# Two decoder layers on one core: products of zeros in TensorE's waits at the seams, a new order for the first stage, and gathers moved ahead at the third stage's start

## What is computed

```
x = x + gated(layernorm(x))                    # layer 0: 1x1 convolutions, 4-tap convolution, silu, softplus
x = x + cross(q=layernorm(x), k=v=ctx)         # 16 heads of 16
x = x + moe32(layernorm(x))                    # 32 experts, top 2, at most 154 rows each, gelu, 256 -> 1024 -> 256
x = x + causal(layernorm(x))                   # layer 1: 16 heads, softmax twice with an entropy-dependent temperature
x = x + mixed(layernorm(x), ctx, phi)          # one head of 256 with a bias from phi
x = x + block(layernorm(x))                    # rms norm, rotary attention, then 8 experts, top 2
```

```python
pos_all = jnp.cumsum(oh, axis=0) - 1
pos = jnp.take_along_axis(pos_all, flat_e[:, None], axis=1)[:, 0]
valid = pos < C
he = jax.nn.gelu(jnp.einsum('ecd,edf->ecf', xe, w1) + b1[:, None, :], approximate=False)
ye = jnp.einsum('ecf,efd->ecd', he, w2) + b2[:, None, :]
y = (y_flat.reshape(T, K, D) * w[..., None]).sum(axis=1)
```

## Time and profile before

| | us |
|---|---|
| median of three runs | 1469.34 (1469.23 to 1470.68) |
| the profiled execution, its own time | 1475.01 |
| its span | 1473.2 |
| TensorE products busy in the span | 1298.6 (88%) |
| TensorE weight loads | 981.8 (67%) |
| VectorE | 781.4 (53%) |
| ScalarE | 687.2 (47%) |
| GpSimd | 534.0 (36%) |
| stage A / barrier into B / barrier into C | 0 to 359.6 / 359.6 / 673.6 |

### The profile page before, as it was taken

How to read it: one execution, slowest core, us unless ns; L and a number is a source line. 1 busy time by engine, 2 the same in 40 slices (tenths; PEclk the granted TensorE clock), 3 DMA queues, 4 the chain that set the end, 5 groups by cost and what they waited for, 6 DMA issues and landing times. The chain is left out here.

```text
span 1473.2 us, 22930 instructions
## 1 busy us (share of the span) xinstructions
PE 1298.6 (88%) x8351; PEld 981.8 (67%) x8390; DVE 781.4 (53%) x1791; ACT 687.2 (47%) x1254; POOL 534.0 (36%) x777
## 2 busy tenths in 40 slices
PE   7898999987999999894667989889888869999996
PEld 6576767766999999893334656656656545666664
DVE  5786868673111111112656687977876645433332
ACT  6464747551322222221446777768767435212211
POOL 2113130302000000004788887877867033322222
PEclk9999999998999999996679999999999989999998
DMA  9674463902877777722100011010010534322221
GB/s 349 252 190 113 120 167 96 233 15 79 290 265 264 264 263 266 291 79 84 36 1 4 12 37 33 12 37 19 1 48 15 228 109 133 58 42 40 45 38 12
DMA packets 70686, 171.00 MB, mean 116 GB/s; under 512 B 8508, under 2 KB 47425, under 8 KB 60464
## 3 DMA queue, kind: packets, MB, share of 16 engines
q1 hardware_dynamic: 54944, 144.39, 30.4%
q0 software_dynamic: 10224, 16.09, 5.2%
q10 hardware_dynamic: 5408, 9.04, 1.7%
HBM read 123.11 MB, written 48.07 MB: 116 GB/s over the span
## 5 line engine op out<-in xcount | busy, mean ns | idle before, releaser
L1174 ACT ACTIVATE b_ht<-ps,b_b 128x154 f32<-128x154 f32 x256 | 85.0, 386 | 203.9 <-PE ps L1141 186.0
L1189 DVE TENSOR_SCALAR b_yt<-ps,b_b 128x154 f32<-128x154 f32 x64 | 21.2, 373 | 245.6 <-PE ps L1154 245.6
L1141 PE MATMUL ps<-b_xet,ring 128*128 128x154 f32 x1024 | 143.6, 298 | 5.3 <-ACT b_ht L1174 5.3
L2350 PE MATMUL ps<-experts,d_xt 128*128 x312 | 147.1, 594 | 1.2 <-ACT d_xt L2406 0.8
L1141 PEld LDWEIGHTS ps<-b_xet,ring 128*128 128x128 f32 x1024 | 138.2, 192 | 5.4 <-issue 5.4
L1154 PE MATMUL ps<-b_ht,ring 128*128 128x154 f32 x1024 | 139.7, 294 | 0.4 <-DVE b_yt L1189 0.4
L1154 PEld LDWEIGHTS ps<-b_ht,ring 128*128 128x128 f32 x1024 | 136.3, 189 | 0.6 <-issue 0.6
L2492 POOL DMA_INDIRECT out_dram<-d_yd,d_to x39 | 60.6, 1554 | 158.4 <-DVE d_yd L2464 146.6
L1623 POOL MEMSET experts<- 128x480 f32 x2 | 1.0, 508 | 318.3 <-POOLq L1084 318.3
L1503 DVE TENSOR_REDUCE c_mx<-ps 128x8 f32<-128x1024 f32 x64 | 77.8, 1216 | 63.5 <-PE ps L1450 63.1
L1466 PE MATMUL ps<-cf,experts 128*128 128x128 f32 x512 | 72.5, 288 | 23.3 <-ACT experts L1536 12.8
(11 more groups left out here) (334 smaller groups left out, 2843.5 us busy)
## 6 DMA issues: line engine op xcount, KB each, us to landing
ring<-in_w SPq DMA_DIRECT2D x64, 1024.0 KB, 5.3
xd<-zero SPq DMA_DIRECT2D x6, 3120.0 KB, 25.6
a_kp<-in_ctx_k SPq DMA_DIRECT2D x8, 1024.0 KB
experts<-in_wd SPq DMA_DIRECT2D x1, 7424.0 KB
d_xd<-xd SPq DMA_DIRECT2D x39, 130.0 KB, 2.1
xe<-zero SPq DMA_DIRECT2D x1, 4928.0 KB, 32.4
b_xe<-xe SPq DMA_DIRECT2D x32, 154.0 KB
ye<-b_ye ACTq DMA_DIRECT2D x32, 154.0 KB
```

Source lines behind the costliest of these rows:

```text
L1141: r = pe.matmul(ps[:, b, CAP * (m % 2):CAP * (m % 2) + CAP], w1r[:, slot, k, P * m:P * m + P], xet[:, e % 2, k, :], start=(k == 0), stop=( ...
L1174: r = a.activation(ht[:, e % 2, m, :], ps[:, b, CAP * (m % 2):CAP * (m % 2) + CAP], ACT.Gelu, bias=b1[:, e, m:m + 1])
L2350: m = pe.matmul(ps[:, b, :], xt[:, j % 2, k, :], w13[:, bass.ds(e, 1), f:f + F1], start=(k == 0), stop=(k == KD - 1))
```

## The change

It has five parts.

1. `keep_warm` issues n products of zeros (128 x 128 by 128 x 256, written to half a PSUM bank that nobody reads) on TensorE: 10 at the program's start, as soon as the zeros are written; 12 at the end of stage A, behind a wait for the last routing's `pr_in`; 12 at the end of stage B; 14 at the start of stage C; in C's first group 3 and 2 ahead of its transposes, behind waits for the combination and for the mean; and 2 each behind the scores of units 1 and 2 of the first group.
2. The table `AT_A` has new numbers. The blocks made ahead now rise in sequence.
3. ScalarE loads the table set with Gelu behind the sixth block made ahead, before it waits for the experts' biases; before, the load stood ahead of the first Gelu.
4. In `AT_C`, `fetch3` of group 0 goes from 5 to 3.7 and `xvi` from 4.7 to 9.8.
5. The pads are written on GpSimd behind `fetch3` of group 1 (`pads_pool`), and ScalarE waits for them at its first `vv` instead of at the start.

```diff
 AT_A = {
...
-    "ak2": (None, None, None, None, None, None, 329.5, None), "ki2": (None, None, None, None, None, None, 331.5, None),
...
+    "ak2": (None, None, None, None, None, None, 340.7, None), "av2": (None, None, None, None, None, None, 342.6, None),
...
@@ phase_a
         program((gated_tensor, cross_tensor), routing_tensor, ahead_tensor)
+        pe.wait_ge(*router.pr_in.at(len(CHOICES) - 1))
+        keep_warm(c, con, 12)
...
+def keep_warm(c, con, n, bank=7):
+
+    for _ in range(n):
+        c.nc.tensor.matmul(c.ps[:, bank, 0:D], con["zero"][:, 0:P], con["zero"][:, 0:D], start=True, stop=True, skip_group_check=True)
@@ phase_b
             ahead.store_sync(n)
+        a.preload_act_table_set("gelu_and_others")
         a.wait_ge(*s_b.at(0))
...
         a.wait_ge(*gl.at(E0 - 1))
+        keep_warm(c, con, 12)
         finish_phase(c)
@@ AT_C
-    "xvi": (4.7, 137.9, None, None, None, None, None, None), "fetch3": (5, 8.8, 19.3, 25.7, 34, 158.2, 169.2, 211.7),
+    "xvi": (9.8, 137.9, None, None, None, None, None, None), "fetch3": (3.7, 8.8, 19.3, 25.7, 34, 158.2, 169.2, 211.7),
@@ causal_tensor, scores(u)
         m.then_inc(*l.sc.up())
+        if woven and g == 0 and 0 < u < 3:
+            keep_warm(c, con, 2, 5)
@@ phase_c
-        def start_pool():
+        def pads_pool():
+            yield AT_C["fetch3"][1] + 0.1
             for l in (one, two):
                 pool.memset(l.vv[:, :, :, HD + 1:32], 0.0)
                 m = pool.memset(l.vv[:, :, :, HD:HD + 1], 1.0)
...
         def start_rest():
+            keep_warm(c, con, 14)
             pe.wait_ge(*w.loaded.at(0))
             pe.wait_ge(*start_in.at(0))
             a.wait_ge(*w.loaded.at(0))
             a.wait_ge(*start_in.at(0))
-            a.wait_ge(*pads.at(0))
@@ first_tensor(g)
             yield at("t0")
+            if g == 0:
+                pe.wait_ge(*comb.at(g))
+                keep_warm(c, con, 3)
+                pe.wait_ge(*first.mean.at(g))
+                keep_warm(c, con, 2)
             pe.wait_ge(*first.xn.at(g))
@@ first_scalar(g)
             a.wait_ge(*vpj.at(g))
-            if g:
+            if g == 0:
+                a.wait_ge(*pads.at(0))
+            else:
                 a.wait_ge(*one.pv.at(g - 1))
@@ phase_c
-        start_pool()
...
-        emit(*whole(pool_program, routing_pool), tiles.pool(begin))
+        emit(pads_pool(), *whole(pool_program, routing_pool), tiles.pool(begin))
@@ build
         v.memset(con["zero"][:, :], 0.0).then_inc(*zero_in.up())
+        nc.tensor.wait_ge(*zero_in.at(0))
+        keep_warm(c, con, 10)
         nc.tensor.wait_ge(*s_in.at(0))
```

More of the change, by code:

```diff
@@ L485 @@
 AT_A = {
[47 rows of a table removed]
-    "choose": (None, 98.8, None, 177.4, None, 257.8, 332.7, 340.7), "gap": (None, 101.4, None, 181.3, None, 261.7, 335, 343.1),
-    "count": (None, 101.8, None, 180.1, None, 260.6, 336.8, 343.9), "weights": (None, 102.8, None, 181.8, None, 262.2, 337.2, 344.7),
[14 rows of a table removed]
[47 rows of a table added]
+    "choose": (None, 95, None, 174.7, None, 255.8, 330.8, 336.6), "gap": (None, 97.6, None, 178.5, None, 259.7, 333.2, 339.7),
+    "count": (None, 97.6, None, 177.3, None, 258.4, 333.2, 340.4), "weights": (None, 98.2, None, 179.1, None, 260.2, 333.8, 341.2),
[14 rows of a table added]
 }
```

## The result

| | before | after |
|---|---|---|
| median (lowest to highest), 4 runs each | 1469.28 (1468.44 to 1470.68) | 1459.51 (1456.01 to 1460.73) |
| profiled execution, its own time / its span | 1475.01 / 1473.2 | 1460.73 / 1458.9 |
| mean granted TensorE clock over the span | 0.955 | 0.965 |

The ratio of the times of after and before is 0.9929, with a 95% interval of 0.991 to 0.9948. By the medians the changed kernel is 9.8 us faster, where -13.6 had been predicted.

What follows compares the result with a forecast made beforehand. TensorE was taken as full or nearly so in stages A, B and the last, with slow-clock stretches behind its waits and needless queueing. Terms -0.4 - 1.8 - 2.5 - 3.0 - 5.9 = -13.6 us gave 1456 from the median 1469.3; range 1446 to 1463.

Steps and rivals of the forecast that it cites:

- Start: Kernel start: ten zero products ahead of the first transposes spare slow first products and delay nothing; -0.4 us (-0.8 to 0).
- Stage A's order: Stage A's second round: the new order removes the slow stretch behind the routing's count, while the wait stays; -1.8 us.
- its end: End of stage A: block 2 behind the last count lets the barrier into B open earlier, less the zero products' price; -2.5 us.
- twelve at 0.24 us are 2.8 us: T + 22.3: First barrier: twelve zero products take 2.8 us, so TensorE arrives last, at T + 22.3; their price is 0.9 us.
- Stage B's start: Behind the first barrier: with zero products the sixth ahead block runs at 2.4 GHz instead of 1.2; -3.0 us (or 0).
- Stage C's start: C's head: own gather fourth, L1860 and pads later, so group 0's normalised rows come earlier; -5.9 us (-3 to -7).
- rival (2): Stage C absorbs its head's gain, since GpSimd sets the pace behind it; 1461.6 us, chance 0.12.
- the rule weighed there: C's head: GpSimd contends with two-input VectorE instructions, so the combination beside gathers would be longer; the sum takes no slowdown.
- (1): Rival: zero products don't hold the clock, losing the 3.0, the 0.4 and 1.6 of the 5.9; 1460.7 us, chance 0.10.
- (3): Rival: the clock stays up through C's head, 3.7 us more; 1452.0 us, or 1448.3 with group 1's projections; chance 0.16.
- (4): Rival: the new order makes TensorE wait for the routing's chain at four places in stage A; +8, 1477 us, chance 0.04.
- (5): Rival: zero products do nothing else, but the order loses 4 to 8 us of the seams' win; 1462 to 1467, chance 0.08.

Runs made afterwards that it cites:

- again: The kernel before, unedited, for a second profile and more times: 1469.18 us, ratio 1.0002 to the kernel before.
- fitted: The changed kernel with fewer zero products: 4 and 6 instead of 12 at the ends of A and B, 10 instead of 14 at C's start: 1458.28 us, ratio 0.9921.
- counts_again: As counts_warm, a second timing: 1459.44 us, ratio 0.9898.
- counts_no_table: counts_warm without loading the Gelu table ahead on ScalarE: 1457.33 us, ratio 0.9898.
- counts_warm: head_warm with five zero products in each of two stage A waits ahead of the routing's count: 1463.4 us, ratio 0.9909.
- order_only: The kernel before with the changed order table AT_A alone: 1472.0 us against 1475.4, ratio 0.9979.
- no_zeros: The changed kernel with all calls of keep_warm taken out: 1460.79 us, ratio 0.9935.
- c_only: The kernel before with stage C's new start alone: 1472.19 us, ratio 0.9978.
- zeros_only: The kernel before with the seven insertions of zero products alone: 1463.81 us, ratio 0.9963.
- head_warm: fitted with more zero products in C's first group, 6 instead of 2 ahead of its transposes and 4 ahead of its first scores: 1469.08 us, ratio 0.9949.
- first set: Four of the twelve follow-up runs, timed together beside the kernel before: again, zeros_only, no_zeros, fitted; ratios 1.0002, 0.9963, 0.9935, 0.9921.
- after_again: The changed kernel, unedited, as yardstick of its set and for a second profile: 1465.66 us, ratio 0.9949.
- counts_fit: fitted with the two times five zero products of counts_warm, without those head_warm added in C's head: 1451.15 us, ratio 0.9856.

## Why the prediction was right, and where it wasn't

The forecast (1456.0, range 1446 to 1463) held, and the sign was right; the sum of -13.6 is 3.8 us more than came. Its parts were further off than its sum. Beside again's profile, which has no stall, the changed kernel's first profile opens the barrier into B 1.0 us earlier, takes 0.9 us less from there to B's last product (307.3 against 308.2) and 6.2 us less from there to the end (792.5 against 798.6). The terms for these were -4.7, -3.0 and -5.9. In the last part zeros cost 2.1 us, so stage C gave 8.3: 4.5 up to ScalarE's L1551 at 944.49 (L1539 at 948.79 in again), and 3.8 behind it, where the change does nothing and where fitted, with the same program there, has none of them (519.2 us to the end; again 518.2, after 514.4). These 3.8 us made up in this profile for a part of what the first two stages lacked, and that was luck. By its own steps:

- **Start, -0.4.** L757's first products come at 23.43 to 23.84 us in the three profiles with ten zeros and at 24.02 to 25.28 in the five without, so the sign stood up and the size, 0.2 to 1.9, differs by execution. But ten products are 20 instructions and end at 8.38 us, later than the transposes' input at 7.5. With six, the row comes at 22.84 in four profiles, another 0.8 us, but at 24.18 and 24.43 in counts_again and counts_no_table, where the clock fell again behind 1.97 and 1.52 us of bare waiting (in counts_warm it didn't behind 1.66). Of this difference nothing is left at the barrier into B, which opens at 350.95 and 351.23 there and at 351.29 in counts_warm. The Trainium skill (TensorE: Matmul & The Clock Gate, Part 1) says that the number of slow products at a kernel's start varies from run to run; the five profiles without zeros there agree.
- **Stage A's order -1.8, and its end -2.5.** The slow stretch behind the first count stayed (the wait is now 3.00 us, not 1.91), and what the first count gained (2.6 us, measured from L757) was gone at the second one. T, the start of the last group's rows, came 0.3 us earlier in place of 2.2. Measured from L757 it stands at 310.6 us in three of the four profiles with the old table (308.9 in the fourth) and at 309.3 to 310.9 in the six with the new one and no zeros ahead of the counts. So the term was 0.3 on average and not 1.8: it failed. For the scatters "block 2 behind the count", 3.45 us, came whole: the last one is 3.9 us earlier. They alone would allow the barrier near 355.7, close to the 355 of the prediction: in fitted it opens 5.3 us behind the last scatter, and in order_only at 356.1.
- **The failed step: "twelve at 0.24 us are 2.8 us: T + 22.3".** A row of eight instructions in the earlier trace rows is four f32 products, since each runs as two instructions. I took it for eight. Twelve are 5.34 us, and they ended at T + 24.5 (353.51 + 5.34 - 334.33), not at T + 22.3. (The line that follows in the prediction, 25.0 - 22.4 = 2.5, should be 25.0 - 22.3 = 2.7.) The same slip is in "twelve zero products end at 673.1, so they hold nothing back": they held the second barrier 2.1 us (first gather 6.1 us behind B's last product, 4.0 in no_zeros, c_only and fitted). Together that is 2.2 + 2.1 us, more than the whole difference of 3.8 us.
- **Stage B's start, -3.0.** The block behind the barrier is 3.75 + 3.15 against 1.96 + 1.89 us: -3.05. But before's second profile had 3.41 and 1.89, so that the term lies between -1.4 and -3.0. And in order_only the block was full without any zeros. The first up product came 3.5 us earlier, not 7 to 8: this sign of the prediction failed, because the barrier came 0.5 us earlier in place of 4.7. **Gelu table, 0:** right.
- **Stage C's start, -5.9.** Right in mechanism and, for the head, in size: from the barrier (671.94) to the combination 8.3 us, where I had given 8 and before had 14.0, and to the rows on ScalarE 13.4 instead of 19.0: -5.6. At the end of the kernel c_only shows 3.2 us (0.6 to 5.9), so rival (2), C absorbs the head's gain, was about half true. Its reason, GpSimd sets the pace, is seen at group 3: its combination starts 31.4 to 31.9 us behind the first gather in nine of the ten profiles with the new start of C, fast head or slow (32.9 in no_zeros). The combination beside gathers took 1.80 us, as in the trace of before. One place does speak for the rule weighed there: group 3's combination runs into a two-input operation of GpSimd and takes 3.24 us instead of 1.80. In before, where that operation comes later, the same combination takes 1.79 us. The prediction looked for this beside the gathers, where it didn't come, and the 1.4 us stand in no term.
```profile
704.01 3.24 DVE L1705 SCALAR_TENSOR_TENSOR x_all<-experts,gwt_all,x_all 128x256 f32<-128x256 f32 x4 [2.36 <-DMA experts<-ye,gidx_all]
...
704.77 1.27 POOL L1747 TENSOR_TENSOR x_all<-x_all,weights 128x512 f32<-128x512 f32 x1
```
- **Rivals.** (1) is refuted by zeros_only. (3) came true in the first profile of after and half in the second, but the 3.7 us that it gave for it didn't come: head_warm shows where they go. (4) and (5) did not come, since order_only is faster than before: the wait ahead of the first count grew by 1.1 us, and the one of 2.76 us that stood ahead of T now stands ahead of the count before it, with 3.1.
- **The parts and the whole.** Zeros alone -0.37%, order alone -0.21%, C's start alone -0.22%: -0.80% in sum, within the interval of the whole (-0.5 to -0.9%). Order and C's start together, in no_zeros, have -0.65% already. So in the changed kernel the zeros add next to nothing, though they are worth 5.4 us in the kernel before. The reason, as far as the traces go: with block 2 behind the count TensorE's wait at the first barrier is only 2.1 us, so there is little clock left to save (1.7 us in no_zeros, nothing in order_only) and no room for 5.34 us of zeros.
- **Spans and medians.** 14.3 us between the two profiled spans, 9.8 between the medians: before's first trace held a stall of 3.4 us that its second and after's first did not; the other 1.1 us are less than the changed kernel's own runs differ by (1456.0 to 1460.7).

## What to carry to other kernels

Work that only keeps an engine busy has to fit the wait: measure one piece of it on the array (an f32 product is two instructions here), and end it ahead of what the wait ends on, since what it overruns at a barrier is lost for every engine. The best place for it was not at the seams but ahead of two small products (the routing's counts) whose slow successors stood on the chain into the barrier: twice five products (2.3 us the first time, 2.4 to 4.1 the second) brought 3.9 us at the barrier (351.0 to 351.3 us in four profiles, 354.8 and 355.2 without), while all the zeros of the changed kernel add nothing measurable to its other parts. A faster piece gives nothing where another chain, here GpSimd's gathers, sets the next step. And a baseline needs two traces before a difference of a few us between spans is explained.

## What the runs showed of the hardware that I had not expected

- Products of zeros hold the granted clock as other products do: behind them, with 0.3 to 0.4 us bare, the first block of stage B took 1.96 to 1.97 us in all nine profiles that have them there.
- Whether the clock falls in a wait of some 2 us varies between executions: behind 2.09 us it was full in order_only (1.96 us for eight) and half in no_zeros (3.49).
- ScalarE stood still for 1.9 to 3.4 us at one and the same instruction of stage C in every profile from two chips (among them after_again and counts_fit) and in before's first; in the four profiles of the first set and in after's first it didn't. The profile names a load of stage A as the releaser, but the wait is for TensorE. In before's first profile the semaphore of the transposes comes at 965.29, 4.4 us behind their modelled end, and that of the product behind them, for which VectorE waits, at 965.34; in after the same transposes end at 953.61 and raise it at 953.63. So TensorE was late there. It was so at up to three more places in the same profiles, in c_only at 846.47, 1090.89 and 1198.35, by 1.6 to 2.9 us. Why is open, and it wasn't tried.
- The kernel before took 1469.6, 1475.4 and 1473.1 us on three chips, more than the 0.1% that four runs on one had suggested; the late products of TensorE are likely a part of it.
- VectorE's combination takes 1.80 us for four beside GpSimd's gathers and up to 3.24 beside a GpSimd operation that reads two inputs.
